# Group norm in token order with the input turned by crossbar DMA, and both heads' hi halves made on ScalarE

## The chip, the core and the metric

The kernel runs on one core of one Trainium2 chip. The metric is the device time of one execution in microseconds (us), lower is better. The kernel before takes 3375.34 us, the median of three runs (3371.14 to 3375.82).

## The reference

The input `x` has 64 images of 14 x 14 tokens with 768 channels, float32. The result is `x + conv(_gn(x))`, with attention inside `conv`:

```python
def _gn(v, G=32, eps=1e-5):                    # per image and group of 24 channels
    g = v.reshape(B, H, W, G, C // G)
    m = mean(g, axis=(1, 2, 4)); s = var(g, axis=(1, 2, 4))
    return ((g - m) / sqrt(s + eps)).reshape(v.shape)
# conv, per image, 12 heads of 64:
qkv = x @ qkv_w.T + qkv_b                      # low-rank terms are added to q and v
attn = (q * 64 ** -0.5) @ k.T                  # 196 x 196 per head
attn += rel_h[..., :, None] + rel_w[..., None, :]    # q times the position tables
out = softmax(attn) @ v
return out @ proj_w.T + proj_b
```

## The kernel before

A first block, `prepare`, loads and turns the weights and splits each into a float16 "hi" part and a float16 "lo" remainder. The second block, `attend`, works on 32 pairs of images. Every product of float32 precision is three float16 products (hi·hi, hi·lo, lo·hi).

Each engine runs a list of steps, written out by hand: `PE_ORDER`, `ACT_ORDER`, `DVE_ORDER`, `POOL_ORDER` and `SP_ORDER` (SP issues DMAs). One pass of a list is a round. An entry `each(kind, old, k)` means: in round q do step k of that kind for pair q − old. A negative `old` is work ahead of time for a later pair. Every engine is strictly in order, so a step that waits holds everything behind it. The first twelve lines of `PE_ORDER` each begin with a score step, S0 to S11, and are called units 0 to 11 here.

The kinds of step, for one pair:

- **LD** loads `x_sb` (98 partitions x 4 x 768, tokens on partitions), issued from ScalarE's queue.
- **X** (6): TensorE turns `x_sb` so that channels lie on partitions, ScalarE copies the result to `xT`, VectorE takes `bn_stats`. **M** and **G** (2): VectorE joins the statistics, and TensorE averages them over a group with the matrix `gmean`; GpSimd makes the power −1/2. **H** (3): VectorE normalizes `xT` in place, ScalarE copies it to `xn_hi`. **L** (3): VectorE makes `xn_lo`.
- **Q, K, V** (6 each): 18 matmuls of 392 columns; ScalarE makes the hi part, VectorE the lo part. **R** (5): the position terms.
- **S** (12, one per two heads and image): TensorE's scores into one PSUM tile, then VectorE's row maximum. **N**: ScalarE's exponentials with row sums, VectorE's reciprocal of them. In the code N on VectorE also makes head 1's hi half of the probabilities (L781). **T**: ScalarE makes head 0's hi half (L690), VectorE makes both lo halves (L789), and SP then issues the crossbar transpose from `split` to `turned`. **P**: TensorE multiplies `turned` by `v_tok` (turned by SP's step **VT**). The next S needs the exponentials of the one before, since there is one score tile.
- **Y** (6): the output projection. **Z** (6): TensorE turns it back, VectorE adds `x` in `y_sb`. SP loads `y_sb` (**LY**) and stores it (**ST**); **CA** and **CB** on SP copy the position terms to `rel_q`, four DMAs each.

The results of Q, K, V, R, X, G, Y and Z go through a PSUM ring of `BANKS = 5` banks in the order of `PE_ORDER` (`PER_PAIR`, `ring_plan`). A step on TensorE waits until the fifth user before it has been read by its last reader (`read[...]`).

## Time and profile before

| | |
|---|---|
| median of the runs | 3375.34 us (3371.14 to 3375.82) |
| the profiled execution's own time | 3373.03 us |
| its span, first to last instruction | 3371.3 us |
| mean granted TensorE clock | 0.991 of full speed |
| TensorE (PE) matmul busy | 3297.2 us, 98% |
| VectorE (DVE) busy | 2528.2 us, 75% |
| ScalarE (ACT) busy | 2098.2 us, 62% |
| GpSimd (POOL) busy | 35.8 us, 1% |

The span is 1.7 us shorter than the execution's own time. Busy time of an engine is the sum of its instructions; a wait is the idle time before an instruction, and its releaser is what ended it. A pair repeats about every 100.5 us, and the rounds between the first and the last look alike.

### The profile page before, as it was taken

The page shows a single profiled execution, that of the slowest core. Times are in us where ns is not written, and L with a number is a line of the kernel's source. Part 1 is how long each engine was busy: PE and PEld are TensorE (multiplying, and loading weights), DVE is VectorE, ACT ScalarE, POOL GpSimd, SP SyncE. Part 2 cuts the span into 40 slices and gives each one's busy share as a digit, 9 for nine tenths or more (in the row PEclk, how much of TensorE's full clock was granted, in tenths as well). Part 3 has the DMA queues.
Part 4 walks back from the last instruction along what each step waited for, and adds up shares of the span by engine and source line. Part 5 has one row for each costly group of instructions (what it writes and reads, how often), then busy time and mean ns, then how long its engine had stood idle before and what let it go on. Part 6 is the DMA issues. An engine that isn't in the chain of part 4 may idle for free.

```text
span 3371.3 us, 80148 instructions
## 1 busy us (share of the span) xinstructions
PE 3297.2 (98%) x31984; PEld 2130.7 (63%) x31984; DVE 2528.2 (75%) x5970; ACT 2098.2 (62%) x5651; POOL 35.8 (1%) x65
## 2 busy tenths in 40 slices
PE   7689999999999999999999999999999999999998
PEld 4456666666666666666666666666666666666665
DVE  7577777777777777777777777777777777777764
ACT  2466666666666666666666666666666666666664
POOL 0000000000000000000000000000000000000000
PEclk9799999999999999999999999999999999999999
DMA  3145664555555556565555555555565555565554
GB/s 128 42 96 109 120 122 103 115 113 112 118 121 107 113 112 114 116 121 107 110 116 113 112 123 118 101 117 111 110 127 120 100 118 108 111 126 122 103 106 105
DMA packets 1091412, 376.13 MB, mean 112 GB/s; under 512 B 916696, under 2 KB 1071320, under 8 KB 1091040
## 3 DMA queue, kind: packets, MB, share of 16 engines
q1 hardware_dynamic: 1075206, 333.63, 49.8%
q10 hardware_dynamic: 15834, 37.37, 3.9%
q8 instruction: 254, 4.16, 0.5%
q14 instruction: 118, 0.97, 0.1%
HBM read 86.60 MB, written 38.54 MB: 37 GB/s over the span
## 4 chain that ended last, share of the span: by engine, by line
PE 94%; DVE 2%; ACT 1%; issue 0%; DMA 0%; POOL 0%; SPq 0%; POOLq 0%; DVEq 0%
PE ring L556 51%; PE ring L623 17%; PE score L599 9%; PE o_ps L613 7%; PE ring L578 3%; PE ring L637 3%; PE ring L629 3%; ACT prob L682 1%; PE ring L642 0%; PE ring L563 0%; DVE split L789 0%; DVE row_max L769 0%; DVE rel_sb L762 0%; DVE split L781 0%; DVE rel_sb L756 0%
## 5 line engine op out<-in xcount | busy, mean ns | idle before, releaser
L556 PE MATMUL ring<-xn_hi,w_hi 128*128 128x392 f16 x3456 | 1143.2, 331 | 4.8 <-DVE xn_lo L839 4.6
L556 PE MATMUL ring<-xn_lo,w_hi 128*128 128x392 f16 x3456 | 1139.8, 330 | 0.0
L556 PE MATMUL ring<-xn_hi,w_lo 128*128 128x392 f16 x3456 | 1139.3, 330 | 0.5 <-issue 0.5
L682 ACT ACTIVATE prob<-score,neg_max,exp_scale 98x196 f32<-98x196 f32 x1536 | 769.8, 511 | 252.9 <-DVE neg_max L773 245.4
L769 DVE TENSOR_REDUCE row_max<-score 98x4 f32<-98x784 f32 x384 | 373.3, 972 | 273.2 <-PE score L599 272.1
L789 DVE SCALAR_TENSOR_TENSOR split<-prob,row_inv,split 98x196 f16<-98x196 f32 x1536 | 545.0, 417 | 7.8
L556 PEld LDWEIGHTS ring<-xn_hi,w_hi 128*128 128x128 f16 x3456 | 342.3, 99 | 260.7 <-issue 7.7
L556 PEld LDWEIGHTS ring<-xn_hi,w_lo 128*128 128x128 f16 x3456 | 338.8, 98 | 237.9 <-issue 3.6
L556 PEld LDWEIGHTS ring<-xn_lo,w_hi 128*128 128x128 f16 x3456 | 338.9, 98 | 208.3 <-issue 1.9
L623 PE MATMUL ring<-o_hi,w_hi 128*128 128x392 f16 x1152 | 380.2, 330 | 1.4 <-DVE o_lo L798 1.4
L623 PE MATMUL ring<-o_lo,w_hi 128*128 128x392 f16 x1152 | 379.8, 330 | 0.0
L623 PE MATMUL ring<-o_hi,w_lo 128*128 128x392 f16 x1152 | 379.6, 330 | 0.0
L690 ACT ACTIVATE split<-prob,row_inv 98x196 f16<-98x196 f32 x768 | 310.3, 456 | 52.9 <-DVE row_inv L777 52.1
L682 ACT ACTIVATION_READ_ACCUMULATOR prob<-score,neg_max,exp_scale 98x1 f32 x1536 | 306.2, 199 | 0.0
L658 ACT ACTIVATE q_hi<-ring,bias 128x392 f16<-128x392 f32 x192 | 112.1, 584 | 297.8 <-PE ring L556 297.8
L777 DVE RECIPROCAL row_inv<-row_sum 98x4 f32<-98x4 f32 x384 | 68.0, 177 | 290.6 <-ACT prob L682 290.6
L613 PE MATMUL o_ps<-turned,v_tok 98*64 98x196 f16 x4608 | 269.5, 252 | 4.0 <-DMA turned<-split 4.0
L701 ACT ACTIVATE yT<-ring,bias,y_scale 128x392 f32<-128x392 f32 x192 | 130.1, 678 | 220.6 <-PE ring L623 220.6
L599 PE MATMUL score<-k_hi,q_hi 64*98 64x196 f16 x1536 | 205.7, 264 | 19.7 <-DVE k_lo L736 12.3
L781 DVE TENSOR_SCALAR split<-prob,row_inv 98x196 f16<-98x196 f32 x768 | 213.0, 320 | 14.3 <-DVE row_inv L777 0.8
L613 PEld LDWEIGHTS o_ps<-turned,v_tok 98*64 98x64 f16 x4608 | 184.8, 109 | 56.1 <-DMA turned<-split 4.3
L697 ACT ACTIVATE o_hi<-o_ps,bias 128x392 f16<-128x392 f32 x192 | 112.7, 587 | 141.3 <-PE o_ps L613 141.3
(118 smaller groups left out, 4896.7 us busy)
## 6 DMA issues: line engine op xcount, KB each, us to landing
y_sb<-in_x SPq DMA_DIRECT2D x192, 196.0 KB
out<-y_sb SPq DMA_DIRECT2D x192, 196.0 KB
x_sb<-in_x ACTq DMA_DIRECT2D x31, 1176.0 KB
rel_q<-rel_sb SPq DMA_DIRECT2D x128, 122.5 KB, 2.4
stage<-in_L_conv_qkv_w SPq DMA_DIRECT2D x3, 2304.0 KB, 15.4
turned<-split SPq DMA_TRANSPOSE x384, 4.2
rel_q<-rel_sb SPq DMA_DIRECT2D x128, 24.5 KB, 1.9
v_tok<-v_split SPq DMA_TRANSPOSE x192, 3.4
```

The costliest lines, as they stand in the source:

```text
L556: last = T.matmul(ring[:, bank, 0:NT], w[:, c, 128 * j:128 * j + 128], xx[:, par, c, :], start=(c == 0 and part == 0), stop=(c == CT - 1 a ...
L599: last = T.matmul(score[0:HALF, head, to], stat[rows, qs], kk[rows, :], start=(part == 0), stop=(part == 3))
L613: last = T.matmul(o_ps[rows, c0:c0 + TOK], v_tok[0:HALF, hp % 2, vv, 2 * image + kh, rows], turned[0:HALF, image, pp, head, :, kh, 0:HALF] ...
L623: last = T.matmul(ring[:, bank, 0:NT], w[:, c, 128 * j:128 * j + 128], oo[:, par, c, :], start=(c == 0 and part == 0), stop=(c == HP - 1 a ...
L658: last = A.activation(to, ring[:, bank, 0:NT], ACT.Identity, bias=bias[:, j:j + 1])
L682: last = A.activation(prob[:, head, half, :], score[0:HALF, head, TOK * half:TOK * half + TOK], ACT.Exp, bias=neg_max[:, k % 2, i:i + 1], ...
L690: last = A.activation(split[0:HALF, k % 2, 0, 0, half, :, 0:HALF], prob[:, 0, half, :].rearrange("p (a k) -> p a k", a=2), ACT.Copy, scale ...
L697: A.activation(o_hi[:, par, hp, :], o_ps[:, 0:NT], ACT.Identity, bias=bias[:, 2 * CT + hp:2 * CT + hp + 1]).then_inc(o_hi_made, 1)
L701: A.activation(yT[:, k % 2, :], ring[:, bank, 0:NT], ACT.Identity, bias=bias[:, 3 * CT + k:3 * CT + k + 1], scale=y_scale[:, :]).then_inc( ...
L769: V.tensor_reduce(row_max[:, k % 2, :], score[0:HALF, :, 0:2 * TOK].rearrange("p a (b k) -> p a b k", b=2), AX.X, ALU.max).then_inc(row_ma ...
L781: last = V.tensor_scalar(split[0:HALF, k % 2, 0, 1, half, :, 0:HALF], prob[:, 1, half, :].rearrange("p (a k) -> p a k", a=2), row_inv[:, k ...
L789: last = V.scalar_tensor_tensor(split[0:HALF, k % 2, 1, head, half, :, 0:HALF], prob[:, head, half, :].rearrange("p (a k) -> p a k", a=2), ...
```

## The change

The group norm is made in token order, on `x_sb` itself. Channels keep their order, so a group is 24 neighbouring channels of a row, and all that works on x works on two of the four token tiles at a time (98 x 1536 elements), k = 0 and 1 being the two images.

- **A** (2, VectorE): sums per group. **G0** (TensorE): `gmean`, now 98 x 98 with the value 1/(24·196), gives the mean on all partitions. **B** (2, VectorE): subtracts it. **U** (2, ScalarE): squares. **D** (2, VectorE): sums of the squares. **G1** (TensorE), the power on GpSimd, **E** (VectorE: a diagonal of the 64 results) and **G2** (TensorE: `ones` times the diagonal) give 1/deviation on all partitions. **H** (2, VectorE): multiplies by it. **I** (2, ScalarE) and **L** (2, VectorE): hi and lo parts into `xs`.
- **XT** (4, SP): crossbar transposes of 112 x 1536 float16 from `xs` to `xn`, from which Q, K and V read their moving columns, as 4 runs of 98 columns, 672 elements apart. The first Q of a pair waits for all four.
- X and M go. A, B and D are spread over an earlier round than E to L.
- ScalarE's T makes the hi halves of both heads; VectorE's N makes only the reciprocal.
- `yT` has one buffer instead of two, `y_sb` two slots instead of three (`YS`). The scratch tile that held `qw_hi` and `qw_lo` is now `xs`, and the squares lie in it too. The five orders are rewritten. In `prepare` the weights are turned without the channel permutation, and the position tables are 32 columns wide instead of 64.

```diff
-YS = 3
+YS = 2
...
+    each("S", 0, 0) + each("P", 1, 10) + each("Z", 2, 5) + each("V", 0, 0) + each("K", 0, 1)
+    + each("S", 0, 1) + each("P", 1, 11) + each("G", -1, 1) + each("V", 0, 1) + each("G", -1, 2) + each("Y", 1, 0)
+    + each("S", 0, 2) + each("P", 0, 0) + each("K", 0, 2) + each("Y", 1, 1) + each("Z", 1, 0)
+    + each("S", 0, 3) + each("P", 0, 1) + each("Y", 1, 2) + each("Z", 1, 1) + each("V", 0, 2)
+    + each("S", 0, 4) + each("P", 0, 2) + each("Z", 1, 2) + each("K", 0, 3) + each("Q", -1, 0)
+    + each("S", 0, 5) + each("P", 0, 3) + each("V", 0, 3) + each("Q", -1, 1)
+    + each("S", 0, 6) + each("P", 0, 4) + each("K", 0, 4) + each("Q", -1, 2)
+    + each("S", 0, 7) + each("P", 0, 5) + each("V", 0, 4) + each("Q", -1, 3)
+    + each("S", 0, 8) + each("P", 0, 6) + each("G", -2, 0) + each("Q", -1, 4, 5)
+    + each("S", 0, 9) + each("P", 0, 7) + each("K", 0, 5) + each("R", -1, 0) + each("Y", 1, 3) + each("R", -1, 1)
     + each("S", 0, 10) + each("P", 0, 8) + each("R", -1, 2, 3, 4) + each("V", 0, 5) + each("Y", 1, 4) + each("Z", 1, 3)
-    + each("S", 0, 11) + each("P", 0, 9) + each("K", -1, 0) + each("X", -2, 0, 1, 2) + each("Y", 1, 5) + each("Z", 1, 4))
...
+    each("Y", 2, 5) + each("U", -1, 1) + soft(0) + each("V", 0, 0)
+    + each("K", 0, 1) + each("P", 1, 11) + soft(1) + each("V", 0, 1)
+    + each("Y", 1, 0) + each("I", -1, 0) + each("N", 0, 2) + each("K", 0, 2) + each("T", 0, 2) + each("I", -1, 1)
+    + each("Y", 1, 1) + each("P", 0, 1) + soft(3) + each("Y", 1, 2)
+    + each("V", 0, 2) + soft(4) + each("K", 0, 3)
+    + each("Q", -1, 0) + each("P", 0, 3) + soft(5) + each("V", 0, 3) + each("LD", -2, 0)
+    + each("Q", -1, 1) + each("N", 0, 6) + each("K", 0, 4) + each("T", 0, 6)
+    + each("Q", -1, 2) + each("P", 0, 5) + soft(7) + each("V", 0, 4)
+    + each("Q", -1, 3) + soft(8) + each("Q", -1, 4)
+    + each("Q", -1, 5) + each("P", 0, 7) + each("N", 0, 9) + each("K", 0, 5) + each("T", 0, 9) + each("R", -1, 0)
+    + each("Y", 1, 3)
+    + each("R", -1, 1, 2) + each("N", 0, 10) + each("R", -1, 3, 4) + each("T", 0, 10) + each("V", 0, 5)
+    + each("Y", 1, 4) + each("U", -2, 0) + each("P", 0, 9) + each("N", 0, 11) + each("K", -1, 0) + each("T", 0, 11))
...
+    each("S", 0, 0) + each("D", -1, 1) + soft(0) + each("V", 0, 0) + each("Z", 2, 4, 5)
+    + each("S", 0, 1) + each("G", -1, 1) + each("K", 0, 1) + each("P", 1, 11) + each("E", -1, 0) + soft(1)
+    + each("G", -1, 2) + each("V", 0, 1) + each("H", -1, 0)
+    + each("S", 0, 2) + each("H", -1, 1) + each("N", 0, 2) + each("K", 0, 2) + each("T", 0, 2) + each("L", -1, 0)
+    + each("S", 0, 3) + each("Z", 1, 0) + each("P", 0, 1) + each("L", -1, 1) + soft(3)
+    + each("S", 0, 4) + each("V", 0, 2) + each("Z", 1, 1) + soft(4) + each("K", 0, 3)
+    + each("S", 0, 5) + each("Z", 1, 2) + each("Q", -1, 0) + each("P", 0, 3) + soft(5) + each("V", 0, 3)
+    + each("S", 0, 6) + each("Q", -1, 1) + each("N", 0, 6) + each("K", 0, 4) + each("T", 0, 6) + each("A", -2, 0)
+    + each("S", 0, 7) + each("Q", -1, 2) + each("P", 0, 5) + soft(7) + each("V", 0, 4) + each("A", -2, 1)
+    + each("S", 0, 8) + each("Q", -1, 3) + each("G", -2, 0) + soft(8) + each("Q", -1, 4) + each("B", -2, 0)
+    + each("S", 0, 9) + each("Q", -1, 5) + each("P", 0, 7) + each("N", 0, 9) + each("K", 0, 5) + each("T", 0, 9)
+    + each("R", -1, 0)
+    + each("S", 0, 10) + each("R", -1, 1, 2) + each("N", 0, 10) + each("R", -1, 3, 4) + each("T", 0, 10) + each("V", 0, 5)
     + each("S", 0, 11) + each("Z", 1, 3) + each("P", 0, 9) + each("N", 0, 11) + each("K", -1, 0) + each("T", 0, 11)
+    + each("B", -2, 1) + each("D", -2, 0))
...
     each("ST", 2, 4) + each("CB", 0, 0) + each("T", 0, 0)
+    + each("VT", 0, 0) + each("ST", 2, 5) + each("LY", 1, 0) + each("T", 0, 1)
+    + each("VT", 0, 1) + each("LY", 1, 1) + each("XT", -1, 0) + each("T", 0, 2)
+    + each("XT", -1, 1, 2) + each("ST", 1, 0) + each("XT", -1, 3) + each("T", 0, 3) + each("LY", 1, 2)
+    + each("VT", 0, 2) + each("ST", 1, 1) + each("T", 0, 4) + each("LY", 1, 3)
+    + each("ST", 1, 2) + each("T", 0, 5) + each("VT", 0, 3) + each("LY", 1, 4)
...
+        xs = S("xs", [128, 2, 4, C], F16)
+        xn = S("xn", [128, 2, 2, 4, CT, ROWS], F16)
...
+        columns = xs[:, :, :, :].rearrange("p a b c -> p (a b c)")[:, 0:2 * HP * NT].rearrange(
+            "p (t a w h) -> p t a w h", t=2, a=HP, w=W)
...
+        squares = xs[0:HALF].rearrange("p a b c -> p (a b c)").bitcast(F32).rearrange("p (b c) -> p b c", b=4)
...
+                elif kind == "XT":
+                    part, image = k // 2, k % 2
+                    wait(sp, xs_lo_made if part else xs_hi_made, 2 * p + image + 1)
+                    sp.sem_inc(sp_go, 1)
+                    sp.dma_start_transpose(xn[:, p % 2, part, 2 * image:2 * image + 2].rearrange("p b c r -> p (b c) r"),
+                                           xs[0:ROWS, part, 2 * image:2 * image + 2].rearrange("r b c -> r (b c)")
+                                           ).then_inc(xn_in, 16)
...
+                        if kind == "Q" and k == 0 and c == 0:
+                            wait(pe, xn_in, 64 * p + 64)
...
-                elif kind == "X":
-                    if k == 0:
-                        wait(pe, x_in, 16 * p + 16)
-                    for i in range(4):
-                        src = x_sb[:, i, :].rearrange("p (a b) -> p b a", b=CT)[:, k, :]
-                        last = T.transpose(ring[:, bank, HALF * i:HALF * i + HALF], src, ident[0:HALF, 0:HALF])
...
+                    if k < 2:
+                        wait(pe, summed, 4 * p + 2 * k + 2)
+                    else:
+                        if p == 0:
+                            pe.wait_ge(ones_made, 1)
+                        wait(pe, diagonal_made, p + 1)
+                    both = sums[:, :, :].rearrange("p n g -> p (n g)")
+                    if k == 0:
+                        last = T.matmul(ring[0:HALF, bank, 0:2 * GROUPS], gmean[:, :], both, start=True, stop=True)
+                    elif k == 1:
+                        last = T.matmul(ring[0:2 * GROUPS, bank, 0:1], both, gmean[:, 0:1], start=True, stop=True)
+                    else:
+                        last = T.matmul(ring[0:HALF, bank, 0:2 * GROUPS], ones[:, :], diagonal[:, :], start=True, stop=True)
+                    last.then_inc(done[kind], 1)
...
+                    for head, made in enumerate((head0_hi_made, head1_hi_made)):
+                        for half in range(2):
+                            last = A.activation(split[0:HALF, k % 2, 0, head, half, :, 0:HALF],
+                                                prob[:, head, half, :].rearrange("p (a k) -> p a k", a=2),
+                                                ACT.Copy, scale=row_inv[:, k % 2, 2 * head + half:2 * head + half + 1])
+                        last.then_inc(made, 1)
...
+                elif kind == "U":
+                    wait(act, centred, 2 * p + k + 1)
+                    if p == 0 and k == 0:
+                        act.wait_ge(xs_zeroed, 1)
+                    wait(act, done["R"], RCH * p)
+                    A.activation(squares[:, two], x_sb[:, two, :], ACT.Square).then_inc(squared, 1)
+                elif kind == "I":
+                    wait(act, normed, 2 * p + k + 1)
+                    two = slice(2 * k, 2 * k + 2)
+                    A.activation(xs[0:HALF, 0, two], x_sb[:, two, :], ACT.Copy).then_inc(xs_hi_made, 1)
...
-                        last = V.tensor_scalar(split[0:HALF, k % 2, 0, 1, half, :, 0:HALF],
-                                               prob[:, 1, half, :].rearrange("p (a k) -> p a k", a=2),
-                                               row_inv[:, k % 2, 2 + half:3 + half], None, ALU.mult)
-                    last.then_inc(head1_hi_made, 1)
...
+                elif kind == "A":
+                    if k == 0:
+                        wait(dve, x_in, 16 * p + 16)
+                    two = slice(2 * k, 2 * k + 2)
+                    V.tensor_reduce(sums[:, k, :], x_sb[:, two, :].rearrange("p b (g c) -> p g b c", c=GP),
+                                    AX.XY, ALU.add).then_inc(summed, 1)
+                elif kind == "D":
+                    wait(dve, squared, 2 * p + k + 1)
+                    two = slice(2 * k, 2 * k + 2)
+                    V.tensor_reduce(sums[:, k, :], squares[:, two].rearrange("p b (g c) -> p g b c", c=GP),
+                                    AX.XY, ALU.add).then_inc(summed, 1)
...
+                elif kind == "E":
+                    wait(dve, inv_dev_made, p + 1)
+                    V.tensor_scalar(diagonal[:, :], ident[0:2 * GROUPS, 0:2 * GROUPS], inv_dev[:, :], None,
+                                    ALU.mult).then_inc(diagonal_made, 1)
...
+                elif kind in ("B", "H"):
+                    wait(dve, read["G"], 3 * p + (1 if kind == "B" else 3))
+                    by_group = x_sb[:, 2 * k:2 * k + 2, :].rearrange("p b (g c) -> p b g c", c=GP)
+                    of = (mean if kind == "B" else rstd)[:, k:k + 1, :]
+                    V.tensor_tensor(by_group, by_group, of.unsqueeze(3).broadcast_to([HALF, 2, GROUPS, GP]),
+                                    ALU.subtract if kind == "B" else ALU.mult
+                                    ).then_inc(centred if kind == "B" else normed, 1)
-                    wait(dve, xn_hi_made, 3 * p + k + 1)
+                    wait(dve, xs_hi_made, 2 * p + k + 1)
                     two = slice(2 * k, 2 * k + 2)
-                    V.tensor_tensor(xn_lo[:, par, two], xT[:, two, :], xn_hi[:, par, two],
-                                    ALU.subtract).then_inc(xn_lo_made, 1)
+                    V.tensor_tensor(xs[0:HALF, 1, two], x_sb[:, two, :], xs[0:HALF, 0, two],
```

## Rows read from the trace of the kernel before

**Rows 1.** The page: shares of the chain that ended last, by engine.

```profile
PE 94%; DVE 2%; ACT 1%; issue 0%; DMA 0%; POOL 0%; SPq 0%; POOLq 0%; DVEq 0%
```

**Rows 2.** Windows: stretch, length, busy PE, PEld, DVE, ACT, POOL, clock, DMA share, GB/s.

```profile
1191.70:1292.20 100.50, 100.50 (x995) 65.05 (x994) 76.84 (x184) 64.69 (x175) 0.69 (x1) 1.00 0.55 113
1306.00:1307.00 1.00, 1.00 (x8) 0.59 (x7) 0.98 (x2) 1.00 (x6) 0.00 (x0) 1.00 0.04 5
```

**Rows 3.** Timeline of TensorE, units 11 to 2: start, us, operation, count.

```profile
1237.39 0.29 PE L599 MATMUL score<-k_hi,q_hi 64*98 64x196 f16 x2
...
1238.83 0.34 PE L556 MATMUL ring<-xn_hi,w_hi 128*128 128x392 f16 x1
...
1241.82 1.75 PE L637 MATMUL ring<-ident,x_sb 98*128 98x98 f32 x12
...
1243.41 0.33 PE L623 MATMUL ring<-o_hi,w_hi 128*128 128x392 f16 x1
...
1246.93 0.29 PE L599 MATMUL score<-k_hi,q_hi 64*98 64x196 f16 x2
...
1260.93 0.28 PE L642 MATMUL ring<-mean_var,gmean 128*128 128x2 f32 x2
...
1261.14 0.29 PE L599 MATMUL score<-k_hi,q_hi 64*98 64x196 f16 x2
```

**Rows 4.** Groups of instructions by form on VectorE and ScalarE: busy us, mean ns.

```profile
L690 ACT ACTIVATE split<-prob,row_inv 98x196 f16<-98x196 f32 x768 | 310.3, 456 | 52.9 <-DVE row_inv L777 52.1
...
L781 DVE TENSOR_SCALAR split<-prob,row_inv 98x196 f16<-98x196 f32 x768 | 213.0, 320 | 14.3 <-DVE row_inv L777 0.8
...
L808 DVE BATCH_NORM_STATS2 stats<-xT 128x6 f32<-128x196 f32 x384 | 112.9, 350 | 18.1 <-ACT xT L708 18.1
...
L839 DVE TENSOR_TENSOR xn_lo<-xT,xn_hi 128x784 f16<-128x784 f32 x96 | 87.6, 968 | 0.0
...
L833 DVE TENSOR_SCALAR xT<-xT,mean,rstd 128x392 f32<-128x392 f32 x192 | 83.4, 477 | 0.9 <-POOL rstd L722 0.9
L712 ACT ACTIVATE xn_hi<-xT 128x784 f16<-128x784 f32 x96 | 80.9, 845 | 9.2 <-DVE xT L833 9.2
```

**Rows 5.** Timeline of VectorE: row maxima of S11, S0 and S7, a reciprocal, lo halves.

```profile
1239.20 0.96 DVE L769 TENSOR_REDUCE row_max<-score 98x4 f32<-98x784 f32 x1
...
1243.81 1.41 DVE L789 SCALAR_TENSOR_TENSOR split<-prob,row_inv,split 98x196 f16<-98x196 f32 x4
...
1247.84 0.97 DVE L769 TENSOR_REDUCE row_max<-score 98x4 f32<-98x784 f32 x1 [1.02 <-PE score L599]
...
1304.15 0.97 DVE L769 TENSOR_REDUCE row_max<-score 98x4 f32<-98x784 f32 x1 [1.54 <-PE score L599]
...
1307.55 0.18 DVE L777 RECIPROCAL row_inv<-row_sum 98x4 f32<-98x4 f32 x1 [0.57 <-ACT prob L682]
```

**Rows 6.** Timeline of the queue of SP, start of a round: ST, CB, T0, VT0.

```profile
1249.70 0.33 SPq L533 DMA_DIRECT2D out<-y_sb  x1
1250.14 2.43 SPq L505 DMA_DIRECT2D rel_q<-rel_sb  x4
1254.38 1.55 SPq L528 DMA_TRANSPOSE turned<-split  x1
1256.13 1.85 SPq L523 DMA_TRANSPOSE v_tok<-v_split  x1
```

**Rows 7.** Landing of the transposes into `turned`, by tile.

```profile
DMA to landing us min/median/max: 4.0/4.2/8.9
```

**Rows 8.** Landing of the transposes into `v_tok`, by tile.

```profile
DMA to landing us min/median/max: 2.7/3.4/6.6
```

**Rows 9.** Timeline of the queue of ScalarE: a load of `x_sb`.

```profile
1297.37 0.32 ACTq L653 DMA_DIRECT2D x_sb<-in_x  x1
```

**Rows 10.** Timeline of TensorE: first X and first Q of the first pair.

```profile
89.73 3.53 PE L637 MATMUL ring<-ident,x_sb 98*128 98x98 f32 x20 [4.25 <-PEq L194]
...
106.18 0.48 PE L556 MATMUL ring<-xn_hi,w_hi 128*128 128x392 f16 x1 [4.62 <-DVE xn_lo L839]
```

208 lines of the change are left out of this document (61 added, 147 removed).

## The prediction

> **What bounds the kernel now.** I read the page's chain first. It lies on TensorE for 94% of the span [rows 1], so only TensorE's own work, or something that makes it wait, can move the time. The windows by pair come next: in a pair's 100.5 us TensorE is busy for 100.5 us, at full clock, while VectorE works 76.8 us and ScalarE 64.7 us [rows 2]. The reader should see two things: there is no idle time left to win, and VectorE has 24 us and ScalarE 36 us a pair in hand on average. An average doesn't say where in the round the slack lies, so the third view is the timeline, engine by engine, around the steps that move [rows 3, 5, 6].
>
> **TensorE's own work.** The starts in [rows 3] give the prices. S and P of a unit take 1238.83 − 1237.39 = 1.44 us, a K (as a Q, V or Y) 1241.82 − 1238.83 = 2.99, three X 1.59. Y and Z together take 1246.93 − 1243.41 = 3.52, so a Z takes 0.53. A G takes 0.21.
> - The six X go: −3.18 a pair. The two G go: −0.42.
> - Three G come. The old ones move 2 columns. The new G0 and G2 move 64 float32 columns, each in two instructions as the old ones. A turn of 98 float32 columns takes 1.59/12 = 0.13, so 64 columns take at most 2 × 0.13 = 0.26 more than nothing. The bounds are 0.63 (three old ones) and 0.95. I take 0.21 + 2 × 0.27 = 0.75, since the loading of weights covers part.
> - Q, K and V read their columns in four runs instead of one. No row shows a Q that does so. The P products read `turned` in two runs, and with the S they take 1.44 us for 14 pairs of 196 columns, 0.10 each against 2.99/18 = 0.17 for 392. That leaves no room for a toll per run; I take nothing, at most 0.5 us a pair.
>
> TensorE's pair becomes 100.5 − 3.18 − 0.42 + 0.75 = 97.65 us, 2.85 less. I count 30 pairs, since the first round is not filled and waits on other engines. That is −85.5 us if TensorE never waits.
>
> Here a rule speaks against the change. The rows say that a turn costs 0.13 us of an engine with nothing to spare. The Trainium skill (VectorE: DVE Perf Modes, Rules for kernel authors) says to turn 128 x 128 blocks on TensorE where PSUM will do as destination and to use the crossbar DMA otherwise. By the row the turns are worth 3.18 us a pair; by the rule they would stay, and of the change only the costs below would be left.
>
> **VectorE and ScalarE in total.** For a pass over 98 x 1536 elements there is no row. A tensor_tensor on 784 takes 0.968 us, as does a row maximum on 784 (0.97). The step from L781 (196, 0.320) to L833 (392, 0.477) costs 0.8 ns an element, that from L833 to L839 1.25 [rows 4, 5]. So 1536 take 1.57 to 1.91; I take 1.75, or 1.67 from one start to the next. On ScalarE L690 (196, 0.456) and L712 (784, 0.845) lead to 1.34 by slope and 1.69 by doubling; I take 1.6.
> - VectorE loses per pair the hi halves 213.0/32 = 6.7, statistics 3.5, the old H 2.6 and L 2.7, and some 1.4 of small operations. It gets 2 each of A, B, D, H, L, 10 × 1.75 = 17.5, and 0.7 of small ones. Net +1.3: 78 of 97.7 us.
> - ScalarE loses the X copies (2.7, an estimate by the size of L712's passes) and L712 2.5. It gets U and I, 4 × 1.6, and 24 hi halves at 310.3/768 = 0.40, 9.7. Net +10.9: 76 of 97.7.
>
> Neither becomes the bound by its sum. The hi halves give VectorE less than 6.7: they were made while ScalarE made head 0's. Now ScalarE makes four at about 0.36 from start to start, and the last lo half ends some 2.45 us after the reciprocal starts, whereas VectorE waits in between. So VectorE's elapsed time per unit stays, and the ten long passes must fit between.
>
> **First place: from S11 to P0.** Count from TensorE's start of S11 (1237.39). VectorE's S11 starts at 1.81, the lo halves of T11 end at 1243.81 + 1.41 − 1237.39 = 7.8 [rows 3, 5]; the R steps ahead, which fill VectorE, stay as they are. Before, S0's scores came at 9.54 and VectorE was waiting for them. Without X they come at 1.44 + 2 × 2.99 + 0.53 = 7.95, ready for VectorE 0.91 later (1247.84 − 1246.93), at 8.9. VectorE then has B1 and D0 in front: 7.8 + 2 × 1.67 = 11.1, which is 2.2 late. From S to its reciprocal 3.4 us pass [rows 5]; D1 lies in that gap. Then 2.45 to the lo halves, 0.5 for V0, 0.7 for Z4: 18.15.
>
> SP's queue has ST of this Z4 in front, then CB, T0, VT0. By [rows 6] CB starts 0.44 after ST and takes 2.43, T0 can go 2.9 after ST, VT0 1.75 after T0. T0 is issued at 21.05 (its halves were done 4 us before) and lands 4.2 later, at 25.25 [rows 7]. VT0 is issued at 22.8 and lands 3.4 later, at 26.2 [rows 8]. TensorE wants both for P0: S0 at 7.95, a unit of 1.44 + 0.5 + 5.98, a unit of the same with two G, and 0.8 for S2's own part: 24.7. **Stall 1.5 us a pair.** V1 on TensorE takes 0.5 of it already, as it needs the bank of Z4 (five users before) at 17.6. Before, VT0 was issued at 1256.13 and its P0 came after 1261.14: over 1.5 us to spare.
>
> **Second place: G0 for the pair after next.** Count from TensorE's S6. VectorE's S6 starts at 0.9, its reciprocal at 4.3. K4 and the longer T6 on ScalarE end the lo halves at 7.35. A0 ends at 9.0, S7 (ready at 8.4) starts then; 3.4 + 2.45 + 0.5 for V4 lead to 15.4, A1 ends at 17.1. TensorE reaches G0, right behind S8 and P6, at 2 × (1.44 + 5.98 + 0.04) + 1.44 = 16.4 (0.04 is what the steps' prices lack per unit to 100.5). **Stall 0.7 us a pair**, with Q4 and Q5 queued behind it. VectorE's lateness here is made up in the R steps, where it waits for ScalarE.
>
> The load of `x_sb` must have landed for A0. It was issued at 1297.37, and at 1306 the DMA engines are all but idle [rows 2, 9], so it needs at most 8.6 us. It is now issued about 2.7 before S6, lands by 5.9, and A0 comes at 7.35: hidden, with 1.4 us to spare. XT goes out at the end of unit 2 and in unit 3. With a landing like that of T, XT3 is in some 3 us before Q0; T2 and T3 behind them on SP stay 3 us ahead of their P. I cost them at nothing.
>
> **The ends.** Before the first Q the new chain is longer. It was 106.18 − 89.73 = 16.45 us [rows 10]. Now: two A 3.4, G0 with copy 0.9, B0 1.75, U0 1.6, D0 and D1 3.4, G1 to G2 2.9, two H 3.4, two L 3.4, XT 3.5, together 24.3: +8 us.
>
> **Sum.** 3371.3 − 30 × 2.85 + 30 × 2.2 + 8 = 3359.8 for the span, and 1.7 around it: 3361.5, say **3361**. The profiled execution of before took 3373.0, 2.3 under the median of its runs, so this is 0.4% below the median.
>
> **Rivals.**
> - *TensorE does not wait.* VectorE's passes are nearer 1.57 than 1.75, and VT0 lands in 2.7, the minimum of [rows 8]. That takes 0.4 + 0.2 and 0.7 off the first stall and 0.3 to 0.5 off the second. For it: all engines but TensorE have over 20% idle. Against it: both chains are serial, and idle time elsewhere doesn't shorten them. Without stalls: 3361 − 66 = 3295. Chance 0.25 for less than 1 us of stall a pair.
> - *As reckoned,* 1 to 2.6 us of stall: 3326 to 3370. Chance 0.38.
> - *It cancels,* 2.6 to 2.9 of stall: within 7 us of 3375. Chance 0.14.
> - *The crossbar comes too late for P0.* VT0 behind T0 and CB, with four XT and two `y_sb` transfers close by, lands nearer the maximum (6.6 and 8.9 in [rows 7, 8]) than the median. From 0.7 us beyond the forecast the kernel is slower; at 6.6 instead of 3.4 the time is 3361 + 30 × 3.2 = 3457, at half of that 3409. A0 held by the load is the same in kind. For it: SP's queue is 4 us late at the start of a round. Against: the median is far from the maximum. Chance 0.23. The rule of the Trainium skill on turns (VectorE: DVE Perf Modes, Rules for kernel authors), cited above, would have this outcome.
>
> Within 0.2% of 3375, about 7 us, a measurement can't tell the kernels apart. So faster 0.63, same 0.14, slower 0.23. The range is 3292 to 3405; the likeliest case's own is 3326 to 3370.
>
> **What would show it.** A pair's period near 99.9 us; `TensorE` waiting about 1.5 us a pair at P0 or V1, released by DMA into `v_tok` or by VectorE's Z, and 0.7 at G0, released by A1; VectorE's S0 starting 3 us or more after TensorE's; T0's issue 3 us after its lo halves; B, D, A near 1.75 us; G0 and G2 near 0.27; Q's matmuls still 0.166 apart; first Q some 24 us after the first step. The prediction is wrong if VectorE reaches S0 in time, if Q's matmuls slow down, or if another wait, above all at Q0 for XT, appears.

## The result and the profile after

The kernel after the change takes **3422.42 us** (median of four runs, 3421.5 to 3423.97). The kernel before, on the same chip, takes 3374.97 us (3371.14 to 3375.82). The ratio on record is 1.0145, interval 1.0133 to 1.0157: 1.45% slower, where 0.4% faster was forecast. (Ratios and intervals are given as recorded for each run; the quotient of the two medians, here 1.0141, can differ from them by up to 0.15%.) The profiled span is 3420.8 us, at a mean granted clock of 0.984.

The page of the kernel after: busy time of TensorE, the chain by engine, DMA queue q1, and three groups with columns as in [rows 4].

```profile
PE 3223.7 (94%) x31280; PEld 2005.0 (59%) x31280; DVE 2562.3 (75%) x4722; ACT 2392.0 (70%) x6259; POOL 35.2 (1%) x65
...
q1 hardware_dynamic: 1251334, 377.69, 58.8%
...
PE 45%; DVE 28%; ACT 15%; issue 4%; DMA 3%; SPq 1%; DVEq 0%; POOL 0%; ACTq 0%; POOLq 0%
...
L797 DVE SCALAR_TENSOR_TENSOR split<-prob,row_inv,split 98x196 f16<-98x196 f32 x1536 | 550.4, 420 | 221.7 <-ACT split L697 220.7
L697 ACT ACTIVATE split<-prob,row_inv 98x196 f16<-98x196 f32 x1536 | 577.2, 450 | 72.8 <-DVE row_inv L788 72.0
L780 DVE TENSOR_REDUCE row_max<-score 98x4 f32<-98x784 f32 x384 | 371.8, 968 | 132.1 <-PE score L597 131.1
```

Two lines of the kernel before, for comparison: q1, and VectorE's lo halves.

```profile
q1 hardware_dynamic: 1075206, 333.63, 49.8%
...
L789 DVE SCALAR_TENSOR_TENSOR split<-prob,row_inv,split 98x196 f16<-98x196 f32 x1536 | 545.0, 417 | 7.8
```

TensorE lost 73.5 us of work (3297.2 before), and the span grew by 49.5. VectorE is no busier than forecast. What changed is the chain: TensorE held 94% of it [rows 1] and now holds 45%. VectorE's lo halves have a new wait of 220.7 us in all, for the hi halves that ScalarE makes; before, they waited 7.8 us.

The window of one pair, columns as in [rows 2]:

```profile
2491.00:2591.80 100.80, 97.84 (x974) 61.10 (x973) 77.83 (x145) 73.85 (x194) 0.54 (x1) 1.00 0.65 127
```

TensorE's work is 97.84 us, as reckoned (97.65), at full clock. Here 2.96 us are idle, where [rows 2] had none. The list of TensorE's waits from 187 to 3200 us says where (sum in us, count, longest):

```profile
PE o_ps L611 <- DMA turned<-split: 24.0, 11, 2.9
PE o_ps L611 <- issue: 22.8, 24, 1.5
PE ring L639 <- DVE sums L817: 21.4, 30, 0.7
PE ring L554 <- DVE y_sb L811: 19.2, 26, 0.8
PE score L597 <- DVE k_lo L747: 6.4, 1, 6.4
PE ring L561 <- DVE xs L750: 5.7, 30, 0.2
```

Four places stall in the pairs: P0 (the first two rows, for the crossbar, but for some 3 us at P10), G0 (for A1), V1 (for Z4's bank), and R0, which needs the lo parts of Q5. The 6.4 us are in the first round alone.

P0's wait is 1.56 us in the mean of rounds 2 to 29. In ten of these rounds it is 1.9 us or more, and in five of the ten TensorE's granted clock falls from 2.4 to 1.2 GHz during P0's wait or within a microsecond of its end, for 20.5 us in all. One such stretch, columns as in [rows 2], behind a wait of 2.7 us:

```profile
2405.50:2412.20 6.70, 6.07 (x28) 3.18 (x29) 2.25 (x4) 2.80 (x9) 0.00 (x0) 0.50 1.00 226
```

The timelines from S11 to P0, first TensorE, then VectorE, then the queue of SP; they answer to [rows 3, 5, 6].

```profile
2482.99 0.29 PE L597 MATMUL score<-k_hi,q_hi 64*98 64x196 f16 x2
...
2490.94 0.29 PE L597 MATMUL score<-k_hi,q_hi 64*98 64x196 f16 x2
...
2501.27 0.50 PE L554 MATMUL ring<-xn,w_hi 128*128 128x392 f16 x2 [0.80 <-DVE y_sb L811]
...
2507.76 0.29 PE L597 MATMUL score<-k_hi,q_hi 64*98 64x196 f16 x2
...
2509.90 0.70 PE L611 MATMUL o_ps<-turned,v_tok 98*64 98x196 f16 x12 [1.26 <-issue]
```

```profile
2490.85 1.75 DVE L841 TENSOR_TENSOR x_sb<-x_sb,mean 98x1536 f32<-98x1536 f32 x1
2492.51 1.75 DVE L822 TENSOR_REDUCE sums<-xs 98x32 f32<-98x1536 f32 x1
2494.18 0.96 DVE L780 TENSOR_REDUCE row_max<-score 98x4 f32<-98x784 f32 x1
...
2497.57 0.18 DVE L788 RECIPROCAL row_inv<-row_sum 98x4 f32<-98x4 f32 x1 [0.51 <-ACT prob L686]
2498.72 1.42 DVE L797 SCALAR_TENSOR_TENSOR split<-prob,row_inv,split 98x196 f16<-98x196 f32 x4 [0.97 <-ACT split L697]
2500.06 0.56 DVE L755 TENSOR_TENSOR v_split<-ring,v_split 128x392 f16<-128x392 f32 x1
2500.54 1.28 DVE L811 TENSOR_TENSOR y_sb<-ring,y_sb 98x512 f32<-98x512 f32 x2
```

```profile
2501.24 0.33 SPq L531 DMA_DIRECT2D out<-y_sb  x1
2501.68 2.43 SPq L496 DMA_DIRECT2D rel_q<-rel_sb  x4
2504.23 1.55 SPq L519 DMA_TRANSPOSE turned<-split  x1
2505.97 1.80 SPq L514 DMA_TRANSPOSE v_tok<-v_split  x1
```

From S11 at 2482.99: VectorE reaches S0 11.19 us later (forecast 11.1), ST goes out at 18.25 (18.15), VT0 at 22.98 (22.8), and TensorE starts P0 at 26.91. The reader should see in VectorE's rows the 0.97 us without work between the reciprocal and the lo halves.

How long the turned columns take to land, by tile: all transposes into `v_tok` (minimum, median, maximum), and VT0 of one late round (issued at 573.1), as in [rows 8].

```profile
DMA to landing us min/median/max: 3.0/3.7/6.9
```

```profile
DMA to landing us min/median/max: 5.5/5.5/5.5
```

The distance between the first score matmuls of neighbouring units, read from TensorE's timeline and averaged over rounds 2 to 29, makes a table in us that the experiments share; under "u2" stands the distance from the start of unit 2 to that of unit 3. The rows from "SP's turns first" on are runs 1, 2, 3, 4, 5, 7, 9, 10 and 12 of the next section. "First S" is the start of the first unit and "rest" what follows the start of the last round.

```
                         u0    u1    u2    u6    u8    u9   u11   pair   first S  rest
before                  6.59  7.63  8.20 10.49  7.51  9.27  9.53  100.56  144.6  115.5
after                   8.09  8.74  9.91  7.51  8.47  9.51  7.94  101.48  160.2  120.8
SP's turns first        8.09  8.68  7.94  7.51  8.47  9.51  7.95   99.51  161.1  121.3
Z behind S0             8.11  9.21  7.95  7.51  8.47  9.51  7.94  100.08  161.8  121.8
G0 behind Q4            8.10  8.69  9.86  7.51  7.65 10.58  7.95  101.66  157.3  121.2
hi half on VectorE      8.11  8.29 10.23  7.51  7.93  9.16  7.95  100.50  160.6  120.5
before, hi on ScalarE   6.59  8.40  8.20 10.49  7.51  9.29  9.53  101.31  143.3  117.2
norm in the gap         8.17  7.98  7.94 10.42  7.72  9.16  7.94  100.70  167.1  122.9
the same, load later    8.14  7.98  7.94  7.51  7.72  9.16  7.95   97.78  160.3  122.8
SP first, hi VectorE    8.07  8.26  7.94  7.51  7.93  9.16  7.94   98.17  160.8  121.5
gap, hi VectorE, power  7.99  7.98  7.94  7.51  7.72  9.16  8.45   98.06  154.1  121.0
```

### The profile page after: what moved, and what is told of

It reads as the page before. It is cut to its first block, busy times and chain, and to the rows that moved or that the text cites. A ratio compares the mean times of both kernels' runs of the same rounds, so it can differ in the third digit from the quotient of the medians.

```text
span 3420.8 us, 78579 instructions
## 1 busy us (share of the span) xinstructions
PE 3223.7 (94%) x31280; PEld 2005.0 (59%) x31280; DVE 2562.3 (75%) x4722; ACT 2392.0 (70%) x6259; POOL 35.2 (1%) x65
## 3 DMA queue, kind: packets, MB, share of 16 engines
q1 hardware_dynamic: 1251334, 377.69, 58.8%
## 4 chain that ended last, share of the span: by engine, by line
PE 45%; DVE 28%; ACT 15%; issue 4%; DMA 3%; SPq 1%; DVEq 0%; POOL 0%; ACTq 0%; POOLq 0%
PE ring L554 23%; PE ring L621 10%; ACT prob L686 9%; DVE split L797 6%; PE score L597 4%; DVE row_max L780 4%; PE o_ps L611 4%; DVE x_sb L841 3%; DVE sums L817 3%; ACT split L697 3%; DMA turned<-split 2%; PE ring L576 2%; DVE rel_sb L773 2%; DVE sums L822 2%; DVE v_split L755 1%
## 5 line engine op out<-in xcount | busy, mean ns | idle before, releaser
L554 PE MATMUL ring<-xn,w_hi 128*128 128x392 f16 x6912 | 1721.5, 330 | 31.8 <-DVE y_sb L811 19.8
L554 PE MATMUL ring<-xn,w_lo 128*128 128x392 f16 x3456 | 1138.1, 329 | 0.0
L554 PEld LDWEIGHTS ring<-xn,w_hi 128*128 128x128 f16 x6912 | 645.6, 97 | 508.7 <-DVE y_sb L811 22.1
L797 DVE SCALAR_TENSOR_TENSOR split<-prob,row_inv,split 98x196 f16<-98x196 f32 x1536 | 550.4, 420 | 221.7 <-ACT split L697 220.7
L697 ACT ACTIVATE split<-prob,row_inv 98x196 f16<-98x196 f32 x1536 | 577.2, 450 | 72.8 <-DVE row_inv L788 72.0
L554 PEld LDWEIGHTS ring<-xn,w_lo 128*128 128x128 f16 x3456 | 333.1, 96 | 246.5 <-issue 6.7
L597 PE MATMUL score<-k_hi,q_hi 64*98 64x196 f16 x1536 | 206.0, 264 | 28.6 <-ACT prob L686 15.2
L747 DVE SCALAR_TENSOR_TENSOR k_lo<-ring,bias,k_hi 128x392 f16<-128x392 f32 x192 | 119.4, 622 | 97.1 <-ACT k_hi L660 97.1
L597 PE MATMUL score<-onehot,rel_q 64*98 64x196 f16 x1536 | 191.4, 245 | 0.0
L597 PE MATMUL score<-k_lo,q_hi 64*98 64x196 f16 x1536 | 191.3, 245 | 0.0
L597 PE MATMUL score<-k_hi,q_lo 64*98 64x196 f16 x1536 | 191.1, 245 | 0.0
```

The source lines that it names most:

```text
L554: last = T.matmul(ring[:, bank, 0:NT], w[:, c, 128 * j:128 * j + 128], xn[:, par, xx, :, c, 0:HALF], start=(c == 0 and part == 0), stop=(c ...
L597: last = T.matmul(score[0:HALF, head, to], stat[rows, qs], kk[rows, :], start=(part == 0), stop=(part == 3))
L697: last = A.activation(split[0:HALF, k % 2, 0, head, half, :, 0:HALF], prob[:, head, half, :].rearrange("p (a k) -> p a k", a=2), ACT.Copy, ...
L747: last = V.scalar_tensor_tensor(lo, ring[:, bank, 0:NT], bias[:, j:j + 1], hi, ALU.add, ALU.subtract)
L797: last = V.scalar_tensor_tensor(split[0:HALF, k % 2, 1, head, half, :, 0:HALF], prob[:, head, half, :].rearrange("p (a k) -> p a k", a=2), ...
```

## Experiments

**1. SP's first turns ahead of the store.** In `SP_ORDER`, T0 and VT0 ahead of ST(2, 4) and CB:

```diff
-    each("ST", 2, 4) + each("CB", 0, 0) + each("T", 0, 0)
-    + each("VT", 0, 0) + each("ST", 2, 5) + each("LY", 1, 0) + each("T", 0, 1)
+    each("T", 0, 0) + each("VT", 0, 0)
+    + each("ST", 2, 4) + each("CB", 0, 0) + each("ST", 2, 5) + each("LY", 1, 0) + each("T", 0, 1)
```

> The changed kernel with SP's queue reordered at the start of a round: T0 and VT0 go ahead of ST of Z4 and of CB. Theory of the queue (P0 waits because VT0 is issued 15.0 us after S0, held in SP's queue behind the store of a Z4 that VectorE makes late): T0 goes out when its halves are ready, about 9.3 us after S0, VT0 at about 11, P0's wait of 1.97 us a pair goes, V1's wait of about 0.8 stays; 3422 becomes about 3363. Rival of contention (the four new crossbar transposes make every transpose land late, whatever the order): P0 still waits 1 us or more a pair for turned or v_tok, and the time stays above 3390.

Measured: 3364.35 us (3362.47 to 3366.61), ratio 0.9975, interval 0.9965 to 0.9985. Unit 2 falls from 9.91 to 7.94 us, the other waits stay, as expected. Of the 1.97 us, 1.56 were P0's wait; the stretches at 1.2 GHz are gone from the pairs too, which account for most of the rest. So the queue of SP ahead of P0 is worth 58 us, and this order alone makes the changed kernel 0.25% faster than the kernel before.

**2. Z4 and Z5 on VectorE right behind S0**, ahead of D1 and the softmax, so that the store and V1's bank come early:

```diff
-    each("S", 0, 0) + each("D", -1, 1) + soft(0) + each("V", 0, 0) + each("Z", 2, 4, 5)
+    each("S", 0, 0) + each("Z", 2, 4, 5) + each("D", -1, 1) + soft(0) + each("V", 0, 0)
```

> The changed kernel with VectorE's Z4 and Z5 moved right behind the row maximum of S0, ahead of D1 and of the softmax of unit 0, as the kernel before has them. Theory of the queue: the ring bank of Z4 is free 6 us earlier, so V1's wait (about 0.8 us a pair) goes, and the store of Z4 leaves SP's queue before T0 is ready, so P0's wait (1.97) goes too; units 1 and 2 take about 8.0 and 8.1 instead of 8.74 and 9.91, and 3422 becomes about 3342. Rival of contention: only V1's wait goes, about 3398. A third way: D1 is now late, the reciprocal of unit 0 waits for it and the wait comes back at S1; then less than 40 us are won.

Measured: 3378.97 us (3372.48 to 3385.81), ratio 1.0019, interval 1.0009 to 1.0028. That is 43 us less than after the change, where the theory had 80. The waits of P0 and V1 are gone. TensorE's waits in the same stretch show what came instead:

```profile
PE ring L643 <- DVE diagonal L830: 29.9, 28, 1.9
```

D1 is later, so the variance and GpSimd's power are, and G2 waits for the diagonal made from it: unit 1 takes 9.21 us. This is the third way of the expectation, a little cheaper than it said.

**3. G0 of the pair after next behind Q4 instead of behind P6**, on TensorE, and its readout on VectorE likewise:

```diff
-    + each("S", 0, 8) + each("P", 0, 6) + each("G", -2, 0) + each("Q", -1, 4, 5)
+    + each("S", 0, 8) + each("P", 0, 6) + each("Q", -1, 4) + each("G", -2, 0) + each("Q", -1, 5)
```

> The changed kernel with G0 of the pair after next moved on TensorE from in front of Q4 to behind it (and its copy on VectorE behind Q4's lo part). Theory of the serial chain: G0 stands there only for A1, which VectorE ends 0.7 us too late; 3 us later the sum is there, unit 8 takes 7.75 instead of 8.47 us, and 3422 becomes about 3400. Rival (VectorE is simply too full there, and the wait moves to the next step that needs it, B0, R0 or S9's row maximum): unit 9 grows by as much, and the time stays within 5 us of 3422.

Measured: 3425.78 us (3418.55 to 3427.92), ratio 1.0154. The wait of G0 is gone and reappears one unit later:

```profile
PE ring L561 <- DVE xs L750: 37.7, 30, 1.3
```

VectorE's lateness is what counts here, not which step meets it.

**4. Head 1's hi half back on VectorE**, all else as after the change:

```diff
+                    for half in range(2):
+                        last = V.tensor_scalar(split[0:HALF, k % 2, 0, 1, half, :, 0:HALF],
+                                               prob[:, 1, half, :].rearrange("p (a k) -> p a k", a=2),
+                                               row_inv[:, k % 2, 2 + half:3 + half], None, ALU.mult)
+                    last.then_inc(head1_hi_made, 1)
```

with the same half taken out of ScalarE's step T. The edit also makes the lo half of head 1 ahead of that of head 0, as the kernel before does; runs 10 to 12 have this too.

> The changed kernel with head 1's hi halves back on VectorE, as the kernel before makes them; all else as changed. Prediction's own view (ScalarE's hi halves free VectorE of 0.28 us each, but VectorE then waits for ScalarE inside each softmax, so its elapsed time per unit stays): VectorE's S0 starts within 0.5 us of where it did, 11.2 us after S11, the stalls stay, and the time is within 10 us of 3422. Rival (the longer work on ScalarE is what makes the lo halves, and so the whole chain, late): the stalls shrink and 20 us or more are won. The other rival (VectorE's busy time counts): VectorE gets 6.7 us a pair more to do, and 20 us or more are lost.

Measured: 3387.19 us (3375.07 to 3392.42), ratio 1.0039, interval 1.0027 to 1.0052: 35 us less. Two groups of this kernel, columns as in [rows 4]:

```profile
L801 DVE SCALAR_TENSOR_TENSOR split<-prob,row_inv,split 98x196 f16<-98x196 f32 x1536 | 545.6, 419 | 8.9
...
L793 DVE TENSOR_SCALAR split<-prob,row_inv 98x196 f16<-98x196 f32 x768 | 213.1, 320 | 14.1 <-DVE row_inv L787 0.5
```

VectorE does 213 us more work and waits 213 us less (8.9 us ahead of the lo halves instead of 221.7). In a plain unit, unit 4, the last lo half ends 2.23 us after the reciprocal's start, against 2.58 with both hi halves on ScalarE. With 0.35 us less a unit the units of V1, G0 and R0 shrink by 0.45, 0.54 and 0.35 us a pair. P0's unit grows by 0.32: its wait is 1.63 us in the mean instead of 1.56, and TensorE stands at 1.2 GHz for 34.1 us of rounds 2 to 29 instead of 20.5.

**5. The kernel before, with both heads' hi halves on ScalarE and nothing else.** The same edit the other way round, the order of the lo halves included.

> The kernel before with only the hi halves changed: ScalarE makes both heads', VectorE only the lo halves. TensorE of the kernel before never waits in a pair, and each softmax has some 3 us in hand before its P, so 0.3 us more in the chain are covered: 3373 within 5 us. Rival (the hi halves on ScalarE cost time by themselves): above 3385.

Measured: 3397.44 us (3397.19 to 3399.73), ratio 1.0075, interval 1.006 to 1.009: 26 us slower, where no change was expected. The waits of TensorE and the lo halves of this kernel:

```profile
PE ring L556 <- DVE y_sb L799: 20.4, 29, 1.0
```

```profile
L785 DVE SCALAR_TENSOR_TENSOR split<-prob,row_inv,split 98x196 f16<-98x196 f32 x1536 | 551.5, 420 | 203.3 <-ACT split L691 202.3
```

My expectation fell. Unit 1 goes from 7.63 to 8.40 us, because K1 needs the bank of Z5 and gets it late. In the old kernel the slack there was 0.06 us: VectorE was done with Z5 7.96 us after TensorE's S0, and K1 started at 8.02. Here the two are 8.72 and 8.78.

**6. One small power on GpSimd ahead of its three memsets**, at the start of `attend`:

```diff
+            pool.wait_ge(minus_half_made, 1)
+            pool.wait_ge(ones_made, 1)
+            G.tensor_tensor(warm[:, :], ones[:, 0:1], minus_half[:, :], ALU.pow)
             G.memset(xs[:, :, :, :].rearrange("p a b c -> p (a b c)"), 0.0).then_inc(xs_zeroed, 1)
```

> The changed kernel with one small power on GpSimd, of ones, put ahead of the three large memsets at the start of the second block. In the changed kernel the first power starts 7.0 us after the last memset although its input has been there since 99.8 us, and in the kernel before it starts 6.9 us after too, with its input just made. Theory A (the first power after a while costs GpSimd some 7 us before it starts, once): that time now passes beside the sums on VectorE; the power that counts starts when its input is there, the first Q comes at about 113 to 116 instead of 118.8, and the time falls by 3 to 6 us. Theory B (the memset itself holds GpSimd for so long, or the delay comes with every switch from memset to power): the first Q stays at 118.8 or comes later, and the time stays at 3422 or above.

Measured: 3425.5 us (3422.75 to 3431.99), ratio 1.016, no gain. The small power itself stands 7.19 us idle first. The next one starts 0.90 us after its input, though memsets lie between. But the memsets now end 8 us later, the squares wait for them, and the first Q is at 120.5.

**7. The norm's steps on VectorE between the reciprocal and the lo halves**, where it waits for ScalarE anyway: A0, A1, B0, B1, D0, L0 and L1 there (two of them shown), Z4 right behind S0, and ScalarE's load of x behind the fourth softmax (unit 4) instead of behind V3 (unit 5).

```diff
-    + each("S", 0, 6) + each("Q", -1, 1) + each("N", 0, 6) + each("K", 0, 4) + each("T", 0, 6) + each("A", -2, 0)
+    + each("S", 0, 6) + each("Q", -1, 1) + each("N", 0, 6) + each("A", -2, 0) + each("K", 0, 4) + each("T", 0, 6)
...
-    + each("S", 0, 11) + each("Z", 1, 3) + each("P", 0, 9) + each("N", 0, 11) + each("K", -1, 0) + each("T", 0, 11)
-    + each("B", -2, 1) + each("D", -2, 0))
+    + each("S", 0, 11) + each("Z", 1, 3) + each("P", 0, 9) + each("N", 0, 11) + each("D", -2, 0) + each("K", -1, 0)
+    + each("T", 0, 11))
```

> The changed kernel with its passes on VectorE at other places of the round, and x_sb loaded one unit earlier: A0, A1, B0, B1, D0, L0, L1 go between the reciprocal of a unit and its lo halves, where VectorE waits 0.97 us for ScalarE anyway (B1 from unit 11 to unit 9), and Z4 right behind S0. The work is the same. Theory of place (the loss is VectorE reaching S0 2.3 us late and A1 ending 0.7 us late, not its amount of work and not the crossbar): S0 is met on time, P0, V1 and G0 no longer wait, a pair takes 97.7 to 98.5 us, and 3422 becomes 3310 to 3335, first power and all. Rival of amount (VectorE with 78 of 98 us and strict order has no room): the waits turn up elsewhere and the pair stays above 99.5, 3360 or more. Rival of contention at the crossbar: P0 still waits 1 us or more.

Measured: 3411.39 us (3383.63 to 3418.68), ratio 1.0104, interval 1.0072 to 1.0135. All four waits are gone, and the commonest round takes 97.5 us. But in unit 6 TensorE now waits for `turned`, 17 times and up to 8.1 us, and such a round takes up to 108 us. Behind these waits the granted clock falls as well: 64.9 us of rounds 2 to 29 are at 1.2 GHz, which by half of it cost some 32 us, an estimate. A bad round: the queue of SP, the load on ScalarE's queue, and TensorE.

```profile
2008.09 1.67 SPq L528 DMA_TRANSPOSE xn<-xs  x1
2009.86 1.95 SPq L521 DMA_TRANSPOSE turned<-split  x1
...
2013.05 1.23 SPq L516 DMA_TRANSPOSE v_tok<-v_split  x1
2014.33 0.56 SPq L533 DMA_DIRECT2D out<-y_sb  x1
2015.83 12.25 SPq L521 DMA_TRANSPOSE turned<-split  x1
```

```profile
2013.39 0.33 ACTq L657 DMA_DIRECT2D x_sb<-in_x  x1
```

```profile
2030.26 1.19 PE L613 MATMUL o_ps<-turned,v_tok 98*64 98x196 f16 x12 [5.05 <-DMA turned<-split]
```

The issue of one transpose takes 12.25 us instead of 1.5. It is the first one behind the 1.2 MB load, which went out 2.4 us ahead of it and 5.3 us behind the last turn of x. Over the 30 rounds the first transpose behind the load takes 1.2 to 13.7 us, median 6.8, and 8 us or more in 13 of them.

The nearest transpose ahead of the load is not a turn of x but VT2, 0.34 us before it here. The wait goes by this distance. Where the load goes out 0.2 to 0.7 us behind VT2, in 22 rounds of runs 7 and 8, the next transpose takes 10.3 to 13.0 us in 21 of them; where it is 0.95 us or more, in 25 rounds, it takes 4.2 to 8.7 us. The distance to the last turn of x does not tell the two apart: at 5.9 us from it, run 7 has a transpose of 12.0 us (VT2 0.66 us ahead of the load) and one of 4.2 (VT2 1.30 us ahead).

**8. The same with a small power in `prepare`**, right behind the memset of `mx` and ahead of GpSimd's reduction over partitions.

> The same as e7_between with one small power on GpSimd in the first block, where GpSimd waits for others for over 30 us. If the first power costs some 7 us once for the kernel, it is hidden there: the power that counts follows its input by about 1 us, the first Q comes 5 to 6 us earlier than in e7_between, and the time falls by as much. If something in between (the reduction over partitions, the memsets) makes GpSimd pay again, there is no difference.

Measured: 3433.44 us (3415.35 to 3447.17). The stalls of run 7 are there too (13 first transposes of 8 us or more), so the time tells nothing of the power. GpSimd's timeline does: the small power took 0.60 us without idle time at 10.6 us, and the one of the first pair, behind the reduction at 55.7 us, still stands 6.59 us idle.

**9. Run 7 with the load back in its place.**

```diff
-    + each("V", 0, 2) + soft(4) + each("LD", -2, 0) + each("K", 0, 3)
-    + each("Q", -1, 0) + each("P", 0, 3) + soft(5) + each("V", 0, 3)
+    + each("V", 0, 2) + soft(4) + each("K", 0, 3)
+    + each("Q", -1, 0) + each("P", 0, 3) + soft(5) + each("V", 0, 3) + each("LD", -2, 0)
```

> The order with the norm's steps between the reciprocal and the lo halves, with one thing taken back: ScalarE's load of the next x is issued again behind the copy of v's fourth tile (unit 5), not behind the fourth softmax (unit 4). Theory: in the run before this one the 1.2 MB load went out 2.4 us ahead of the turn of unit 4's probabilities, while the four turns of x were still being written, and SP's issue of that one turn took 4.4 to 13.7 us in place of 1.5; with the load 8 us later the turn takes its 1.5 to 3 us again, unit 6 falls from 10.4 to 7.5 us, the pair from 100.7 to 97.7, the first matmul on normed x comes at 119 in place of 127 (there the load was ahead of the turns of x), and the time is 3411 - 30 x 3 - 8 = 3313 us, 3300 to 3330. Rival: it is the new place of the sums and not the load that makes the turn late; then unit 6 stays near 10 us and the time is near 3400.

Measured: **3313.0 us** (3312.51 to 3313.93), ratio 0.9822, interval 0.9808 to 0.9837. Unit 6 is at 7.51 us in the mean. The load again lies 2.35 us ahead of the next transpose, as in run 7, but the last turn of x went out 14 us before, and the last transpose of any kind, T4, 5.6 us before:

```profile
2045.52 2.40 SPq L528 DMA_TRANSPOSE xn<-xs  x1
...
2061.84 2.63 SPq L521 DMA_TRANSPOSE turned<-split  x1
```

```profile
2016.00:2113.00 97.00, 97.00 (x965) 60.71 (x963) 77.02 (x143) 73.29 (x194) 0.54 (x1) 1.00 0.65 132
```

In that window TensorE is busy for all of its 97.00 us, with the same work on VectorE and ScalarE as after the change. No first transpose behind the load takes more than 2.66 us. Ahead of the first pair the same holds: the first Q is at 118.6, against 127.0 in run 7, where the load went out at 114.4, among the four turns of x (110.98 to 121.9).

**10. SP's order of run 1 and head 1's hi half on VectorE of run 4, together.**

> Two edits that were each run alone, together: SP's first turns ahead of the store and the copy of the bias rows (3364 alone), and the hi halves of head 1 back on VectorE (3387 alone). Theory: they take away different waits (the first those of P0 and V1's bank, 2.0 us a pair; the second those of G0, the bank of R0 and half of that of y, 1.0 us a pair and more), so the gains add: 3422 - 58 - 35 = 3329 us, 3315 to 3340. Rival: the hi halves on VectorE make its Z4 and the store earlier anyway, and both edits take the same wait of P0; then the time is that of the better one, 3355 to 3365.

Measured: 3323.7 us (3322.88 to 3324.42), ratio 0.9854, interval 0.9839 to 0.9868. The kernel is 99 us under the one after the change, where the two gains of 58 and 35 make 93: they add. No stretch at 1.2 GHz is left in rounds 2 to 29, of which run 4 still had 34.1 us.

**11. Run 10 with the small power right behind the reduction over partitions.**

```diff
             G.partition_all_reduce(top[:, :], mx[:, :], 128, RMAX).then_inc(reduced, 1)
+            step(G.tensor_tensor(warm[:, 2:3], warm[:, 0:1], warm[:, 1:2], ALU.pow))
```

> The kernel of the run before with one more operation: GpSimd does one small power right behind its reduction over partitions at 56 us, where it then idles until 88 us. Theory: the 7 us that the first power stands idle in (98.6 to 105.6 us after the change, 7.2 us where it was put ahead of the three memsets, 6.6 us where a small power had run ahead of the reduction over partitions and not behind it) are paid once behind that reduction; paid at 56 us they are hidden, and the first matmul on normed x comes 5 to 6 us earlier, with the time 5 to 6 us below the run before. Rival: the memsets themselves or something else at 88 us bring it, and first matmul and time stay as they are.

Measured: 3317.76 us (3316.34 to 3318.93), ratio 0.9835: 5.9 us less. GpSimd's timeline:

```profile
55.66 0.40 POOL L293 PARTITION_ALL_REDUCE top<-mx  x1 [45.17 <-DVE mx L345]
63.29 0.59 POOL L294 TENSOR_TENSOR warm<-warm 128x1 f32<-128x1 f32 x1 [7.24 <-issue]
...
99.85 0.55 POOL L737 TENSOR_TENSOR inv_dev<-var_eps,minus_half 64x1 f32<-64x1 f32 x1 [1.35 <-DVE var_eps L834]
```

The 7 us are paid at 56 us, where GpSimd has nothing to do, and the first Q moves from 118.8 to 113.0.

**12. The order of run 9, hi half on VectorE, small power behind the reduction.**

> The order of the first run of this batch with the hi halves of head 1 on VectorE too and the small power behind the reduction. Theory: with the load back in its place nothing waits in the pair in either, so it stands at 97.5 us a pair like the first run of this batch, with 5 to 6 us less ahead of the first pair: 3300 to 3315 us. Rival: with the hi halves on VectorE its work of a unit (18.0 of 7.5 to 10 us units at 1.75 us a norm step) overruns the units with a sum in them, and the pair is 98.5 us or more: 3335 us or more.

Measured: 3315.94 us (3315.72 to 3319.11), ratio 0.9833. It begins 6 us earlier than run 9 and is not faster: the pair takes 98.06 us, since unit 11 takes 8.45. S0 waits there for the lo part of K0, which VectorE ends 8.35 us after S11 in the mean and 7.75 in run 9. Ahead of it stand D0 and now the two hi halves: with the steps already in the gap, the hi half on VectorE has no idle time to fill. The result lies between my two expectations, nearer the rival's mechanism.

## Why the prediction was wrong

**TensorE's own work: right.** 97.65 us a pair were forecast. Run 9 has next to no wait in the pairs (0.13 us, at P10) and takes 97.78, or 97.5 in its commonest round. Q's matmuls are still 0.166 us apart, so four runs of columns cost nothing. G0 and G2 take 0.26 us a matmul. The passes over 98 x 1536 take 1.75 us, as chosen.

**The miss in parts.** The span was forecast at 3359.8 and came out at 3420.8. I take the distances of the table against run 9's, which has the same work and next to no stalls.

- The 31 periods from first S to last S0: −19.5 us forecast, +28.6 measured. A pair takes 101.48 and not 99.85, 1.63 more.
- Up to the first S: +15.6 instead of +8.
- From the last round's start: +5.3, which the sum did not have: 3.4 between its S0 and S11 and 1.9 behind.

The three misses, 48.1, 7.6 and 5.3, make up the 61.0.

**First place, from S11 to P0: the term that failed in the sum.** The mechanism was right, the size too small. "Stall 1.5 us a pair" came out at 2.73: V1's unit is 0.76 us longer than in run 9 (8.74 − 7.98), P0's 1.97 (9.91 − 7.94). In the round shown the two waits are 0.80 and 1.26, 2.06 in all. Against the forecast VT0 goes out 0.2 us later, lands in 3.8 and not 3.4, and P0 starts 0.1 after that, 0.7 in all; TensorE would be there 0.15 later (26.91 − 2.06 = 24.85). Of the other 0.67 some 0.3 is a longer wait at P0, 1.56 in the mean: in 13 of 29 rounds T0 takes 4.6 to 6.4 us to land, VT0 up to 5.5, and P0 waits up to 2.9. I had put medians into a chain with no cover at its end. These landings are skewed (VT0's lowest is 3.6, its median 3.7, its highest 5.5), so the late ones are not made up by early ones. The last 0.36 is the clock, which the forecast did not have: 20.5 us at 1.2 GHz instead of 2.4 cost half of that, 10.2 us in 28 pairs. Run 1 shows that all of P0's wait comes from the order on SP. There T0 goes out 9.3 us after S0's start on TensorE and not 13.3, it lands in 4.1 to 4.7 us in every round, and the clock stays up.

**VectorE and ScalarE in total: a step that failed, though little of it is in the 61.0.** "So VectorE's elapsed time per unit stays" put the move of the hi halves at nothing. It does not stay: 2.58 us from reciprocal to last lo half instead of 2.23 in a plain unit. VectorE gave up 213 us of work and got as much idle time, in a place where nothing else was queued to use it. By run 4 that is 35 us in the changed kernel, by run 5 26 us in the old one. What TensorE pays for it is V1 0.45, G0 0.54 and R0 0.35 a pair, less the 0.32 of P0's unit: 1.0 us a pair. The forecast worked both its chains with 2.45 us, so it had most of V1's and G0's part in its stalls, and laid them to the long passes of the norm. What failed is the account of where they come from: 1.0 of the 3.7 us that a pair takes more than in run 9 is the price of this second edit, which the forecast took for free. Missing from the sum were only R0's part and 0.13 us a unit (2.58 − 2.45).

**Second place, G0: right for the kernel as it is.** 0.7 us was forecast, 0.71 measured: A1 ends 17.1 after S6, and TensorE is there at 16.5. The forecast left out R0's wait for the lo parts of Q5, by which unit 9 is 0.35 us longer, as it held that VectorE makes up its lateness in the R steps; it does, but one step too late. Run 3 shows both as one lateness.

**The ends.** 24.3 us were forecast from the first step to the first Q; 30.8 were measured (88.06 to 118.85). GpSimd's power, 5.8 us late, and the four turns of x, 4.6 us from the last L to the first Q instead of 3.5, carry the difference:

```profile
105.60 0.59 POOL L734 TENSOR_TENSOR inv_dev<-var_eps,minus_half 64x1 f32<-64x1 f32 x1 [7.02 <-issue]
```

```profile
118.85 0.83 PE L554 MATMUL ring<-xn,w_hi 128*128 128x392 f16 x2 [11.67 <-DMA xn<-xs]
```

Its input was there at 99.8 and it started at 105.60. Before, GpSimd stood idle for 6.9 us ahead of its first power as well, but the input was only made at the end of them, and VectorE waited 0.9 us. The first step started 1.7 us earlier than the first X did before, so the first Q is 4.8 us behind the forecast. The other 2.8 of the 7.6 lie between first Q and first S, where TensorE's mean granted clock is 0.83 of full speed, against 0.90 before:

```profile
118.85:160.20 41.35, 30.26 (x301) 17.64 (x301) 24.23 (x29) 16.43 (x25) 0.00 (x0) 0.83 0.15 43
```

```profile
106.18:144.60 38.42, 30.11 (x311) 18.19 (x311) 19.09 (x31) 14.74 (x26) 0.00 (x0) 0.90 0.17 46
```

As to the power, run 11 shows its idle time to be a cost paid once behind the reduction over partitions. The Trainium skill (GPSIMD Engine Reference, 2.1 Instruction dispatch) says that the first call of a freshly loaded routine costs about 6 us with no instruction in the profile. The traces agree in kind, with a little more, 6.6 to 7.2 us. That it is the loading of a routine no run here shows, only that it is paid once and behind the reduction.

**The rivals.** The crossbar too late for P0 (chance 0.23, 3409 to 3457) has the right time, and part of the right cause. P0 and V1 went 1.23 us a pair over the forecast; the rival needed 0.7 beyond it for "slower". Landings, the rival's cause, are some 0.7 of it, an estimate (the median 0.3 over the forecast's, and the late rounds, which alone put P0's wait from 1.1 in most rounds to 1.56 in the mean); 0.36 is the clock. R0's 0.35, the ends and the clock were in no rival, so it is in part luck that the time falls into this one's stretch. The rule of the Trainium skill cited with it (VectorE: DVE Perf Modes, Rules for kernel authors: turn on TensorE where PSUM will do) had the outcome of the change as it stands. For the crossbar itself these runs do not bear it out: with the same turns on the crossbar runs 9 to 12 are 1.5% to 1.8% faster than the kernel before. What TensorE was rid of, 2.8 us a pair, is all there once nothing waits.

**Open.** Why T0 and VT0 land late in some rounds and not in others was not settled. With the store and CB behind them (run 1) T0 does not take more than 4.7 us; which of the two does it was not tried apart. Nor was it settled what exactly holds the transpose behind the load in run 7. That the load's place decides it is shown by runs 7 and 9 in the pairs, and by their first Q ahead of them. Whether the turns of x or the transpose just ahead of the load are what counts, no run varies by itself; the distances in runs 7 and 8 point at the latter.

## What to carry to other kernels

When work moves off an engine with idle time, ask whether another step stands ready in the place that it leaves. If the engine then waits there for the work's new owner, each later step is as late as before or later, and the busy time saved is worth nothing. Put the long passes of another pipeline into that gap: here, with Z4 also moved right behind S0, it took 109 us off the changed kernel (run 9). Moving a load one unit earlier at the same time lost 98 of them again (run 7).

Where a chain through a DMA queue ends at a busy engine with no time to spare, count the spread of its landings and not the median. Look first at what is queued ahead of the late transfer: two entries moved ahead on SP's queue were worth 58 us. And a wait of TensorE can cost more than its length: behind some of P0's waits the granted clock fell to half.

## What the runs showed of the hardware

- A crossbar transpose that is issued 2.4 us behind a 1.2 MB load on another queue holds its queue for 4.2 to 13.7 us instead of 1.5, if another transpose went out up to 1.3 us ahead of the load (runs 7 and 8). With the same lead and 5.6 us since the transpose ahead of the load it took 1.5 to 2.7 us (run 9).
- TensorE's granted clock fell from 2.4 to 1.2 GHz in five of the ten rounds in which P0 waited 1.9 to 2.9 us, for 20.5 us in all (rounds 2 to 29 after the change). In run 1, where P0 doesn't wait, it did not fall in rounds 2 to 29.
- The first power on GpSimd after its reduction over partitions starts 6.6 to 7.2 us after the instruction ahead of it, with no instruction in between. Ahead of the reduction it did not pay this, and later powers, behind memsets too, don't.
- Transposes into `v_tok` of the same size land in 3.0 to 6.9 us, median 3.7, against 3.4 before the change, with q1's share of the DMA engines at 58.8% instead of 49.8%.
